# Layer 0's expert block: GpSimd's scalings and weighted sums cut into pieces that stand singly behind indirect transfers

## The chip, the cores and the metric

The kernel runs on one core of one Trainium2 chip. The metric is the device time of one execution in microseconds (us). The engines are TensorE (PE, with PEld for its weight loads), VectorE (DVE), ScalarE (ACT), GpSimd (POOL) and SyncE (SP), which issues the plain transfers. GpSimd issues the indirect ones, which send rows to places in DRAM given by a list of indices, or fetch them from there.

## The reference, cut to what matters

Two layers, each an attention part and a mixture of experts. The change touches only layer 0's experts and the normalisation behind them:

```python
h = _layernorm(x) * (1 + cb) + sb
x = x + gb * _L0_ffn_ref(h, ...)
# _L0_ffn_ref: router logits -> softmax -> top 2 of 8 experts; each expert is
# 128 -> 512, gelu, 512 -> 128; the result is the weighted sum of the two experts' rows
# layer 1 begins with
h = _layernorm(x) * (1 + ca) + sa
```

x has 4 batches of 1024 tokens with 128 channels.

## The kernel before, in words

Every engine has its own program; they meet at semaphores. The first block, `front`, does layer 0's attention, the router and the sort. Its order is written out by hand in `FRONT_ORDER`: each engine walks the same list and executes the stages that it has. GpSimd's last stages there are `sd.1.6` to `sd.1.15`, the last sends of batch 1, one indirect transfer each (line 158). VectorE's last ones are `be.1` (the choice of the two best experts), `gates`, `ix.1` (row numbers) and `te.1` (the expert of each tile), lines 767 to 823.

The second block, `experts0`, works through 92 tiles of 128 sorted rows, 23 for each of 4 batches, in 23 steps of 4 (`UNROLL`). For a tile

- SP loads the rows of 4 tiles at once (line 1292) once `rows_here` says that their batch has been sent,
- PE transposes them (line 1422), ACT copies them out (line 1399),
- DVE copies the tile's expert's up weights to a fixed place, four tiles ahead (`bring_up`, line 1335, 128x512 fp32 from SBUF to SBUF),
- PE multiplies up (line 1428), DVE adds the bias (line 1340), ACT applies gelu (line 1406), PE multiplies down (line 1435), DVE adds the second bias into `y_rows` (line 1349) and raises `y_ready`,
- SP stores two tiles of `y_rows` at once (line 1286); when the store has landed it raises `y_free`.

Beside this GpSimd works through a list of its own (lines 1307 to 1327). Batches 0 and 1 have been sent in `front` (`SENT_EARLY` is 2). For batch 2 and then batch 3 it scales and shifts the batch's normalised rows in two operations of 128x1024 (lines 149 and 151) and sends them in 16 indirect transfers (line 158). Then, for batches 0, 1 and 2, it waits until SP has stored the batch's tiles (`y_free`), fetches the rows with 16 indirect transfers (`gather`, line 1207), and, for batches 0 and 1, does the weighted sum in five operations of 128x1024 (`weighted_sum`, lines 1708 to 1723). Batch 3 is fetched, and batches 2 and 3 are summed, in the block that follows.

The transfers are paced by `next_tile`: it counts a tile number up and waits until that tile's `y_rows` are done. Its number never falls behind a batch's start:

```python
def next_tile():
    tile_at[0] += 1
    pool.wait_ge(y_ready, tile_at[0] + 2)
```

So a transfer that comes late does not wait at all, and neither do those behind it until the count has caught up.

Once a batch is summed (`summed`), DVE computes the statistics of its rows for layer 1's normalisation in two unrolled steps that begin at step `STATS_AT` (13 for batch 0, 20 for batch 1), and GpSimd raises the variance to the power -1/2 (`invert`, line 1691), which it does between transfers of the following batch. A block ends when all engines have ended.

## Time and profile before

| | us |
|---|---|
| median of 3 runs | 1414.41 (1411.29 to 1415.12) |
| profiled execution, its own time | 1412.28 |
| its span | 1410.6 |
| block `experts0` in the trace | about 186 to 403 |
| first and last tile's `y_rows` (line 1349) | 196.68 and 400.23 |

Times in the rows are microseconds from the span's start. In a timeline row the first number is the start, the second the duration; in square brackets stands the idle time of the engine before it, and what ended it. A windows row gives a stretch, its length, and the busy time of PE, PEld, DVE, ACT and POOL, each with its number of instructions, then the granted clock of TensorE (1.00 is full speed), the DMA engines' busy share and GB/s. DMA_INDIRECT is an indirect transfer's issue on GpSimd, not its landing.

### The profile page before, as it was taken

The numbers are of one execution on the slowest core, as the hardware profiler recorded it, in microseconds if no ns is written. First come the engines' busy times: TensorE is split into PE (matmuls) and PEld (weight loads), VectorE is DVE, ScalarE is ACT, GpSimd is POOL, SyncE is SP. The second block draws the span as 40 slices with busy tenths as digits, with TensorE's granted clock in tenths as the row PEclk, the third lists the DMA queues.
The fourth block names the chain that finished last, engine by engine and source line by source line (L and its number), as shares of the span: only waits on it lengthen the run. The fifth ranks groups of instructions, "written<-read, shape, count | busy, mean of one in ns | idle before, by whom it ended". The sixth has DMA issues, their size and how long they took to land. (4 is left out here: it accounts for less than half of the span.)

```text
span 1410.6 us, 28627 instructions
## 1 busy us (share of the span) xinstructions
PE 1275.9 (90%) x9145; PEld 817.9 (58%) x9146; DVE 1030.0 (73%) x2720; ACT 918.1 (65%) x1320; POOL 511.8 (36%) x608
## 2 busy tenths in 40 slices
PE   6999768989886778999999999998999989998999
PEld 3877668988863423333334433333434357778898
DVE  5656266667568669888888878888988857787554
ACT  4565523333355487888888878888888848774232
POOL 5337835466449242222201222220122200388800
PEclk9999779999988799999999999999999989999999
DMA  8980112332316722222222222222022014011211
GB/s 258 222 53 24 36 58 87 97 80 72 85 53 232 201 46 37 43 41 39 32 34 33 41 39 41 42 35 38 24 42 37 9 48 139 17 57 57 71 35 32
DMA packets 112673, 93.96 MB, mean 67 GB/s; under 512 B 20034, under 2 KB 98336, under 8 KB 112544
## 3 DMA queue, kind: packets, MB, share of 16 engines
q1 hardware_dynamic: 101192, 76.18, 25.0%
q0 software_dynamic: 6144, 12.73, 3.1%
q10 hardware_dynamic: 5208, 3.43, 1.0%
q8 instruction: 69, 1.13, 0.4%
q14 instruction: 60, 0.49, 0.1%
HBM read 50.40 MB, written 41.89 MB: 65 GB/s over the span
## 5 line engine op out<-in xcount | busy, mean ns | idle before, releaser
L2446 ACT ACTIVATE probs<-scores_ps 128x1024 f32<-128x1024 f32 x512 | 507.2, 1027 | 86.2 <-PE scores_ps L2473 81.5
L2473 PE MATMUL scores_ps<-q_pack,k_pack 64*128 64x512 f32 x1024 | 246.6, 494 | 36.1 <-ACT probs L2446 21.2
L2490 PE MATMUL pv_ps<-probs,v_pad 128*32 128x512 f32 x2048 | 275.9, 611 | 0.0
L2473 PEld LDWEIGHTS scores_ps<-q_pack,k_pack 64*128 64x128 f32 x1024 | 96.2, 185 | 309.6 <-issue 153.5
L2366 POOL TENSOR_TENSOR squares<-sparse_scores 128x512 f32<-128x512 f32 x32 | 41.0, 1280 | 474.2 <-DVE sparse_scores L2611 474.1
L1406 ACT ACTIVATE hidden_experts<-pre_experts 128x512 f32<-128x512 f32 x94 | 59.3, 631 | 130.2 <-DVE pre_experts L1340 66.5
L2683 DVE TENSOR_SCALAR_CACHE_REDUCE junk<-sparse_scores,at 128x1024 f32<-128x1024 f32 x96 | 122.8, 1279 | 3.4
L1428 PE MATMUL up_ps_experts<-x_t_experts,up_weights_now_experts 128*128 128x128 f32 x752 | 108.2, 289 | 16.4 <-issue 7.7
L1428 PEld LDWEIGHTS up_ps_experts<-x_t_experts,up_weights_now_experts 128*128 128x128 f32 x752 | 96.1, 200 | 22.6 <-DVE up_weights_now_experts L1335 11.1
L1435 PE MATMUL down_ps_experts<-weights_t,hidden_experts 128*128 x736 | 100.5, 281 | 0.2 <-issue 0.2
L1435 PEld LDWEIGHTS down_ps_experts<-weights_t,hidden_experts 128*128 128x128 f32 x736 | 92.7, 198 | 0.0
L3278 POOL DMA_INDIRECT expert_rows_dram<-expert_input_tail,send_to_tail x64 | 63.4, 991 | 79.9 <-DVE send_to_tail L3406 61.4
L1340 DVE TENSOR_TENSOR pre_experts<-up_ps_experts,weights_t 128x512 f32<-128x512 f32 x94 | 64.5, 687 | 34.8 <-PE up_ps_experts L1428 26.4
L3607 ACT ACTIVATE hidden_tail<-up_ps_tail,weights_t 128x160 f32<-128x160 f32 x128 | 41.0, 394 | 67.3 <-PE up_ps_tail L3746 61.6
L158 POOL DMA_INDIRECT expert_rows_dram<-expert_input,pick x64 | 64.0, 1000 | 51.9 <-DVE y_rows_experts L1349 31.7
L2490 PEld LDWEIGHTS pv_ps<-probs,v_pad 128*32 128x32 f32 x2048 | 40.5, 108 | 64.9 <-issue 63.8
L2539 PE MATMUL misc_ps<-sparse_v,sparse_w_t 128*128 (+1 forms) x480 | 69.5, 288 | 0.0
L2539 PEld LDWEIGHTS misc_ps<-sparse_v,sparse_w_t 128*128 128x128 f32 x480 | 58.1, 191 | 14.3 <-issue 14.3
L2611 DVE TENSOR_SCALAR_CACHE_REDUCE sparse_scores<-misc_ps 128x1024 f32<-128x1024 f32 x32 | 39.2, 1224 | 27.2 <-PE misc_ps L2510 27.1
L1335 DVE COPY up_weights_now_experts<-weights_t 128x512 f32 x96 | 57.6, 603 | 1.6 <-PEq L453 1.4
L3778 PE MATMUL out_ps_tail<-gated_out_pieces_tail,place_tail 128*128 128x128 bf16 x960 | 57.5, 221 | 0.0
L3778 PEld LDWEIGHTS out_ps_tail<-gated_out_pieces_tail,place_tail 128*128 128x128 bf16 x960 | 56.1, 99 | 0.6
(416 smaller groups left out, 2493.0 us busy)
## 6 DMA issues: line engine op xcount, KB each, us to landing
q_pack<-q_pieces_dram SPq DMA_DIRECT2D x120, 64.0 KB
k_pack<-k_pieces_dram SPq DMA_DIRECT2D x120, 64.0 KB
expert_rows_dram<-zeros SPq DMA_DIRECT2D x1, 6400.0 KB, 23.0
x_rows_experts<-expert_rows_dram SPq DMA_DIRECT2D x25, 256.0 KB
expert_rows_dram<-y_rows_experts SPq DMA_DIRECT2D x46, 128.0 KB
q_pieces_dram<-q_pieces_prep SPq DMA_DIRECT2D x8, 512.0 KB, 3.6
k_pieces_dram<-k_pieces_prep SPq DMA_DIRECT2D x8, 512.0 KB, 4.1
expert_rows_dram<-zeros SPq DMA_DIRECT2D x1, 2640.0 KB, 40.0
```

The lines of the kernel that those rows point to most:

```text
L158: pool.indirect_dma_start(self.rows, bass.IndirectOffsetOnAxis(ap=g.pick0[:, b, k, n : n + 1], axis=0), self.h[:, b * NT + n, :], None).th ...
L1340: dve.tensor_tensor(pre[:, k % 2], up_ps[k % 2][:], up_bias(e).unsqueeze(2).to_broadcast([P, FC, P]), ALU.add).then_inc(pre_ready, 1)
L1406: act.activation(hidden[:, k % 2], pre[:, k % 2], ACT.Gelu).then_inc(hidden_ready, 1)
L1428: ins = pe.matmul(up_ps[k % 2][:, c, :], up_now[:, k % UNROLL, c, :], x_t[:, k % UNROLL, :], start=True, stop=True)
L1435: ins = pe.matmul(down_ps[k % 2][:, 0:C], hidden[:, k % 2, c, :], down_w(e, c), start=(c == 0), stop=(c == FC - 1))
L2446: act.activation(probs[:, kt % 2, 2 * pair : 2 * pair + 2, c * 512 : c * 512 + 512], scores_ps[n % 2][:].rearrange("p (h t) -> p h t", h=2 ...
L2473: ins = pe.matmul(scores_ps[n % 2][:, head * 512 : head * 512 + 512], k_pack[group % 2][rows, pair, kt * P : kt * P + P].bitcast(F32R), q_ ...
L2490: ins = pe.matmul(pv_ps[32 * j : 32 * j + 32, c, :], v_pad[:, group % 2, kt, j, :], probs[:, kt % 2, j, c * 512 : c * 512 + 512], start=(k ...
L2539: ins = pe.matmul(misc[:, 0:C], w_t[:, n, :], f.sparse_v[:, bass.ds(b * NT + n, 1), :].rearrange("p n c -> p (n c)"), start=(n == 0), stop ...
L2683: step(dve.tensor_scalar(junk[:], s[:, t, :], at[:, t : t + 1], None, ALU.is_ge, ALU.add, accum_out=count[:, t : t + 1]))
L3278: pool.indirect_dma_start(expert_rows.rows, bass.IndirectOffsetOnAxis(ap=send_to[:, b, k, n : n + 1], axis=0), n3[:, b % 3, n, :], None).t ...
L3778: ins = pe.matmul(out_ps[h][:, i * C : i * C + C], place[:, (b * SLOT_TILES + t) % PLACES, n * P : n * P + P], pieces[:, (b * MIX_PARTS + ...
```

## The change

Batch 2's scaling and shifting moves to the end of `front`, in 8 pieces of 128x256 (`hq.2.0` to `hq.2.7`, behind `sd.1.15`). Batch 3's, in 8 such pieces, stands behind the first 8 sends of batch 2. The weighted sums are made of half batches: 10 operations of 128x512 for each batch. Batch 0's ten stand behind fetches 1 to 10 of batch 1. Of batch 1's ten, 8 (`ADDED_FIRST`) run in a row once batch 1 has been fetched, and two stand behind fetches 0 and 1 of batch 2. The fetches of batch 2 are paced from tile 76 (`LAST_FROM`). The statistics of batch 0 move from step 13 to step 17. Both `invert` operations move behind the last fetch and its pacing wait. Batch 1's fetches get a semaphore of their own.

```diff
+QUARTERS = 4
+    def scale_and_shift_part(self, pool, step, b, i):
+        at = b * NT + i % QUARTERS * (NT // QUARTERS)
+        h = self.h[:, at : at + NT // QUARTERS, :]
+        if i == QUARTERS:
+            step.settle()
+        op, by = ((ALU.mult, CB), (ALU.add, SB))[i // QUARTERS]
+        step(pool.tensor_tensor(h, h, bc(self.mod0[:, b, MOD0_PARTS.index(by), :], NT // QUARTERS), op))
...
-sd.1.12 sd.1.13 sd.1.14 sd.1.15 wk.10 ce2.3.1 ...
+sd.1.12 sd.1.13 sd.1.14 sd.1.15 hq.2.0 hq.2.1 hq.2.2 hq.2.3 hq.2.4 hq.2.5 hq.2.6 hq.2.7 wk.10 ce2.3.1 ...
...
+                def scale_and_shift_part(b, i):
+                    if i == 0:
+                        for h in range(2):
+                            wait_made(pool, "tu2", b, h)
+                    moe.scale_and_shift_part(pool, step, b, i)
...
-    STATS_AT = (13, 20)
+    STATS_AT = (17, 20)
+    ADDED_FIRST, LAST_FROM = 8, 76
...
                     if b >= SENT_EARLY:
-                        moe.scale_and_shift(pool, step, b)
                         step.settle()
-                        moe.send_rows(g, pool, b, apart=next_tile)
+                        for i in range(SEND_PARTS):
+                            moe.send_rows(g, pool, b, i, SEND_PARTS, apart=next_tile)
+                            if b + 1 < B and i < 2 * QUARTERS:
+                                moe.scale_and_shift_part(pool, step, b + 1, i)
...
-                for b in range(B - 1):
-                    pool.wait_ge(y_free, b * (2 * AHEAD) + (2 * AHEAD + 1))
-                    tile_at[0] = max(tile_at[0], (b + 1) * moe.tiles)
-                    gather(pool, g, picked, b, [(k, n) for k in range(2) for n in range(NT)], g.rows_picked, apart=next_tile)
-                    if 1 <= b <= EARLY:
-                        pool.wait_ge(var_ready, b)
-                        g.ln1.invert(pool, b - 1).then_inc(rstd_ready, 1)
-                    pool.wait_ge(g.rows_picked, (b + 1) * (16 * 2 * NT))
-                    if b < EARLY:
-                        for part in weighted_sum(g, picked, b, NT):
-                            part(pool, step)
+                sums = [weighted_sum(g, picked, b, NT // 2) for b in range(EARLY)]
+                def add_up(b):
+                    sums[b].pop(0)(pool, step)
+                    if not sums[b]:
                         pool.sem_inc(summed, 1)
+                def fetch(b, sem, of, behind):
+                    for i, (n, k) in enumerate([(n, k) for k in range(2) for n in range(NT)]):
+                        gather(pool, g, picked, b, [(k, n)], sem)
+                        next_tile()
+                        if i in behind:
+                            if of == 0 and i == behind[0]:
+                                pool.wait_ge(g.rows_picked, 16 * 2 * NT)
+                            add_up(of)
+                    if behind:
+                        tile_at[0] += 1
+                pool.wait_ge(y_free, 2 * AHEAD + 1)
+                tile_at[0] = max(tile_at[0], moe.tiles)
+                fetch(0, g.rows_picked, None, ())
+                pool.wait_ge(y_free, 2 * (2 * AHEAD) + 1)
+                tile_at[0] = max(tile_at[0], 2 * moe.tiles)
+                fetch(1, g.second_picked, 0, range(1, 11))
+                pool.wait_ge(g.second_picked, 16 * 2 * NT)
+                for _ in range(ADDED_FIRST):
+                    add_up(1)
+                pool.wait_ge(y_free, 3 * (2 * AHEAD) + 1)
+                tile_at[0] = max(tile_at[0], LAST_FROM)
+                fetch(2, g.rows_picked, 1, range(10 - ADDED_FIRST))
+                for b in range(EARLY):
+                    pool.wait_ge(var_ready, b + 1)
+                    g.ln1.invert(pool, b).then_inc(rstd_ready, 1)
+                pool.wait_ge(g.rows_picked, 2 * (16 * 2 * NT))
                 pool.wait_ge(rstd_ready, EARLY)
```

## Rows read from the trace of the kernel before

**Rows 1.** The page, busy time of each engine over the span

```profile
PE 1275.9 (90%) x9145; PEld 817.9 (58%) x9146; DVE 1030.0 (73%) x2720; ACT 918.1 (65%) x1320; POOL 511.8 (36%) x608
```

**Rows 2.** Windows, three stretches of the expert block

```profile
228.00:250.00 22.00, 18.16 (x141) 17.33 (x140) 12.79 (x24) 6.41 (x11) 12.95 (x11) 0.92 0.25 75
250.00:297.00 47.00, 46.84 (x413) 46.31 (x412) 30.58 (x74) 19.03 (x31) 22.70 (x24) 1.00 0.37 99
...
356.00:375.00 19.00, 15.04 (x107) 14.51 (x106) 7.66 (x18) 5.42 (x9) 9.62 (x10) 0.82 0.25 68
```

**Rows 3.** Timeline, `y_rows` of tiles 16, 24, 48, 54, 58, 64, 72, 78

```profile
228.28 0.29 DVE L1349 TENSOR_TENSOR y_rows_experts<-down_ps_experts,down_bias 128x128 f32<-128x128 f32 x1 [0.42 <-SPq L1294]
...
250.05 0.29 DVE L1349 TENSOR_TENSOR y_rows_experts<-down_ps_experts,down_bias 128x128 f32<-128x128 f32 x1 [0.47 <-SPq L1294]
...
296.77 0.29 DVE L1349 TENSOR_TENSOR y_rows_experts<-down_ps_experts,down_bias 128x128 f32<-128x128 f32 x1 [0.48 <-SPq L1294]
...
311.59 0.29 DVE L1349 TENSOR_TENSOR y_rows_experts<-down_ps_experts,down_bias 128x128 f32<-128x128 f32 x1 [0.93 <-issue]
...
326.55 0.29 DVE L1349 TENSOR_TENSOR y_rows_experts<-down_ps_experts,down_bias 128x128 f32<-128x128 f32 x1 [0.55 <-SPq L1294]
...
338.26 0.29 DVE L1349 TENSOR_TENSOR y_rows_experts<-down_ps_experts,down_bias 128x128 f32<-128x128 f32 x1 [0.46 <-SPq L1294]
...
356.23 0.29 DVE L1349 TENSOR_TENSOR y_rows_experts<-down_ps_experts,down_bias 128x128 f32<-128x128 f32 x1 [0.54 <-SPq L1294]
...
375.07 0.29 DVE L1349 TENSOR_TENSOR y_rows_experts<-down_ps_experts,down_bias 128x128 f32<-128x128 f32 x1 [0.88 <-SPq L1294]
```

**Rows 4.** Timeline, VectorE's operations beside GpSimd's, in both blocks

```profile
88.93 2.35 POOL L149 TENSOR_TENSOR expert_input<-expert_input,mod 128x1024 f32<-128x1024 f32 x1
...
89.39 1.91 DVE L752 SCALAR_TENSOR_TENSOR 0b_minus_mean_rstd_front<-ln0b_mean_var_front,ln0b_rstd_front 128x4 f32<-128x4 f32 x1
...
227.47 2.36 POOL L149 TENSOR_TENSOR expert_input<-expert_input,mod 128x1024 f32<-128x1024 f32 x1 [1.43 <-DMA expert_rows_dram<-expert_input,pick]
...
228.49 1.62 DVE L1335 COPY up_weights_now_experts<-weights_t 128x512 f32 x1
```

**Rows 5.** Windows, line 1335 alone, sum over 296.9 to 308 and 338 to 350.5

```profile
sum 23.60, DVE 15.33; mean DVE 7.67
```

**Rows 6.** Timeline, first and fifth of five sends in a row, and VectorE

```profile
232.61 1.01 POOL L158 DMA_INDIRECT expert_rows_dram<-expert_input,pick  x1 [0.28 <-POOL expert_input L151]
...
237.72 0.96 POOL L158 DMA_INDIRECT expert_rows_dram<-expert_input,pick  x1 [0.30 <-issue]
...
239.85 0.69 DVE L1340 TENSOR_TENSOR pre_experts<-up_ps_experts,weights_t 128x512 f32<-128x512 f32 x1 [3.48 <-remote]
```

**Rows 7.** Timeline, first of seven fetches in a row, and VectorE

```profile
356.28 1.04 POOL L1207 DMA_INDIRECT v<-expert_rows_dram,pick  x1 [6.98 <-SPq L1294]
...
363.55 0.29 DVE L1349 TENSOR_TENSOR y_rows_experts<-down_ps_experts,down_bias 128x128 f32<-128x128 f32 x1 [2.96 <-remote]
```

**Rows 8.** Timeline, the end of `front` and the block's first matmul

```profile
185.16 0.19 DVE L823 TENSOR_SCALAR tile_expert<-expert_front 128x46 int32<-128x46 f32 x1
...
186.08 2.33 POOL L149 TENSOR_TENSOR expert_input<-expert_input,mod 128x1024 f32<-128x1024 f32 x1 [9.68 <-POOLq L453]
...
188.72 1.11 PE L1422 MATMUL xt_ps_experts<-ident,x_rows_experts 128*128 128x128 f32 x4 [8.44 <-DMA x_rows_experts<-expert_rows_dram]
```

**Rows 9.** Timeline, GpSimd's operations of 128x512 and 128x256 elsewhere

```profile
505.36 1.04 POOL L2368 TENSOR_TENSOR squares<-squares 128x512 f32<-128x512 f32 x1
506.48 0.73 POOL L2370 TENSOR_TENSOR squares<-squares 128x256 f32<-128x256 f32 x1
```

**Rows 10.** Timeline, the end of the expert block

```profile
388.58 1.68 POOL L1691 TENSOR_TENSOR ln_rstd<-ln_var_eps,minus_half 128x8 f32<-128x8 f32 x1 [2.48 <-DVE ln_var_eps L1687]
...
400.23 0.29 DVE L1349 TENSOR_TENSOR y_rows_experts<-down_ps_experts,down_bias 128x128 f32<-128x128 f32 x1
...
403.18 0.24 DVE L1695 SCALAR_TENSOR_TENSOR ln_minus_mean_rstd<-ln_mean_var,ln_rstd 128x8 f32<-128x8 f32 x2 [2.32 <-PEq L1269]
```

More of the change, by code:

```diff
@@ L195 @@
 lg.2.1 wk.18 wt.8 lgk.2.1 h2t.3.0 wt.7 wt.4 wk.8 lg.3.0 wk.7 wt.14 lgk.3.0 wk.12 wk.14 wk.4 rs2.3.1 sd.1.6 sd.1.7 sd.1.8 sd.1.9 sd.1.10 sd.1.11
-sd.1.12 sd.1.13 sd.1.14 sd.1.15 wk.10 ce2.3.1 no2.3.1 tu2.3.1 h2t.3.1 lg.3.1 lgk.3.1 be.1 po.1 exps gates ix.1 te.1
+sd.1.12 sd.1.13 sd.1.14 sd.1.15 hq.2.0 hq.2.1 hq.2.2 hq.2.3 hq.2.4 hq.2.5 hq.2.6 hq.2.7 wk.10 ce2.3.1 no2.3.1 tu2.3.1 h2t.3.1 lg.3.1 lgk.3.1 be.1 po.1 exps gates ix.1 te.1
 """
@@ L635, in _ @@
                         h2=scale_and_shift,
+                        hq=scale_and_shift_part,
                         sd=send,
@@ L1482, in __init__ @@
         self.rows_picked = a.sem("rows_picked")
+        self.second_picked = a.sem("second_rows_picked")
         self.zeros = a.sb("zeros", [P, C])
```

## The prediction, made before the changed kernel was run

> **What bounds the kernel now.** The page comes first: TensorE is busy for 90% of the span and GpSimd for 36% [rows 1], so GpSimd's work costs time only where it makes others wait. Next the windows over the expert block. Between 250 and 297 us, where GpSimd only issues transfers, PE is busy for 46.84 of 47 us at full clock: the stretch is PE's. Between 228 and 250 PE lacks 3.8 us and between 356 and 375 4.0 us, and its clock is at a mean of 0.92 and 0.82 there [rows 2]. So the block has places where PE is kept waiting.
>
> To size them I count tiles by VectorE's `y_rows`. Tiles 24 to 48 take 296.77 - 250.05 = 46.72 us, or 1.947 us a tile; this is the pace with paced transfers beside it [rows 3]. Against it:
>
> - tiles 16 to 24: 21.77 us for 15.57, **6.2 lost**. Batch 3's two scalings stand at its start, five sends in a row behind them.
> - tiles 48 to 54: 14.82 for 11.68, **3.15 lost**, beside batch 0's weighted sum; tiles 54 to 58: 14.96 for 7.79, **7.15 lost**, beside nine fetches in a row.
> - tiles 64 to 72: 17.97 for 15.57, **2.4 lost**, beside batch 1's weighted sum.
> - tiles 72 to 78: 18.84 for 11.68, **7.15 lost**, beside seven fetches in a row, which begin when SP's store lets GpSimd go [rows 3, 7].
>
> That is 26.05 us in four places. Two things cost them, and the timeline separates them.
>
> *A long operation of GpSimd holds VectorE.* The copy of up weights takes 1.62 us from 228.49; it ends 0.28 us after GpSimd's operation that began at 227.47 and took 2.36 [rows 4]. A copy that starts while GpSimd computes waits for the end of that one operation and slips in ahead of the next. Beside the two sums 11 copies take 15.33 us, 1.39 each instead of 0.42 [rows 5], and the tiles lose (3.15 + 2.4) / 11 = 0.50 us: 0.97 of delay costs 0.50, so some 0.45 is swallowed. By length, ten whole operations of 2.36 us cost 5.55 us, 0.235 us for each us of GpSimd's computing. The two scalings come to 2 x 2.36 x 0.235 = 1.1 us by this, which leaves 6.2 - 1.1 = 5.1 us for the five sends.
>
> *A run of transfers goes with a stall.* From 232.61 to 237.72 five sends start 1.28 us apart, and VectorE stands for 3.48 us for "remote", until 239.85 [rows 6]; in the run of seven it stands for 2.96 us until 363.55 [rows 7]. All three runs of five or more in this block have this, the runs of three or fewer don't. I can't name the mechanism, only the coincidence. TensorE's clock is low behind each one, part of the price.
>
> **The change, part by part.**
>
> *Batch 3's scaling in pieces behind batch 2's sends.* What stood at 227.47 goes, and with it the reason for the run of five: GpSimd comes to batch 3's sends on time and paces them. Minus 6.2. In its place 8 pieces of 128x256 come in tiles 0 to 8. One takes 0.73 us and a gap of 0.08, the distance between the end of one operation and the next [rows 9]; a send with its gap takes 1.28 [rows 6]. Together 2.09 us for a tile of 1.947, so GpSimd falls 1.1 us behind over 8 and catches up with two or three sends in a row. A piece meets a copy in a third of the tiles and holds it for half its length: 0.15 us on average, less than is swallowed. I take +0.5 in all, bounds 0 and, by length, 8 x 0.73 x 0.235 = 1.4.
>
> *Batch 2's scaling moved to the end of `front`.* GpSimd is idle there for 9.68 us before 186.08 [rows 8], and 8 x 0.81 = 6.5 us fit, so GpSimd isn't late. The cover isn't free, though. In these same 9 us VectorE goes through the chain of small operations that ends at 185.16 and ends the block [rows 8]. A small operation with two inputs in SBUF took 1.91 us from 89.39 and ended 0.02 us after GpSimd's operation of 2.35 us [rows 4]. If each two-input operation waits so for a piece, and one of them slips in between two, the chain can be walked by the code's list: six pieces each catch one operation of `be.1`, which then ends 2.5 us late (the reductions between them run freely), and two more meet the first of `gates`. The chain ends 3.1 us late. Bounds: 0 if VectorE gets through, 8 x 0.73 = 5.8 if it waits for every piece in full. I take +3.1. What goes at the head of `experts0` saves nothing: there PE waits 8.44 us for the rows' load, until 188.72 [rows 8], not for the copies.
>
> The Trainium skill, in "SBUF — State Buffer", section on the two physically separate sides, says that the port pair shared by VectorE and GpSimd is an exclusive lock held for a whole instruction, and that a VectorE operation with two SBUF inputs takes part. By this rule the term is 3.1, and it speaks against putting the pieces under that chain; the one row alone would also allow a value near 0.
>
> *Batch 0's weighted sum in ten pieces behind batch 1's fetches.* The sum at 296 goes (-3.15) and the run of nine behind it (-7.15). A piece of 128x512 takes 1.04 [rows 9] to half of 2.36, 1.18 [rows 4]; with gaps ten make 12 us, and ten fetches 12.8: 24.8 us for ten tiles of 19.5. Batch 1's fetches also begin some 2 us behind tile 47, because the store of its rows must land. So at the tenth piece GpSimd is 7 us, more than three tiles, behind, and fetches 11 to 15 follow each other without pause: a fetch gains 0.67 us on a tile, not enough for the pacing to return before the last. **A run of five is left.** The nearest row is the run of five sends, 5.1 us; bounds 0 and the 7.15 of the run of seven. I take +5.1. The pieces themselves: GpSimd computes half of the time, so a copy waits 0.3 us on average, and 0.45 is swallowed; I take +1.0 for ten tiles, bounds 0 and, by length, 11.8 x 0.235 = 2.8.
>
> *Batch 1's sum, eight pieces in a row, two behind fetches.* Minus 2.4. Nine us of pieces lie over 5 tiles; a copy waits half a piece, 0.6 us, instead of 0.97. By what is swallowed that is 0.15 a tile, by length 0.45; I take +1.2 with the two later pieces, bounds 0.3 and 2.8. Is `summed` in time? Piece 9 starts with tile 76's `y_rows`, then a fetch, then piece 10: 0.3 + 1.3 + 1.3 + 1.3 = 4.2 us, tile 78.2. VectorE asks in tile 80, over 3 us later: no wait.
>
> *Batch 2's fetches paced from tile 76.* They begin at the same store, but after the first one GpSimd waits for tile 76, and then one tile each: the run of seven is gone. Minus 7.15. What is late next is the last fetch: it goes out with tile 90 and lands before the block's end.
>
> *Both powers at the end.* GpSimd now waits for the last `y_rows`, 400.23 + 0.29, is released some 0.3 later, and does two powers of 1.68 us: 404.2 [rows 10]. Before, the last store ended the block: 2.66 us from the end of `y_rows` to VectorE's next operation at 403.18 [rows 10]. The passage from one block to the next takes some 0.5 us, if I take the one before, from 185.35 to 186.08, less GpSimd's start [rows 8]. So the block ends at 404.7: **+1.5**, bounds 0.9 and 2.2.
>
> *Statistics at step 17 instead of 13*: the same operations on VectorE in other tiles, `summed` long there (about tile 62, asked at 68). Nothing. SP's list isn't touched.
>
> **Sum.** Removed 6.2 + 10.3 + 2.4 + 7.15 = 26.05. Added 3.1 + 0.5 + 5.1 + 1.0 + 1.2 + 1.5 = 12.4. Gain 13.65 against the profiled execution's own 1412.28: 1398.6. That execution lies 2.1 us under the median of the runs shown, so I say **1399**.
>
> **Rivals.**
>
> 1. *The remaining run of five is free.* For it: the next block fetches twelve in a row without a "remote" wait. Against: three of three in this block. 1394.
> 2. *Pieces cost by their length.* 8 x 0.73 + 20 x 1.18 = 29.4 us of pieces at 0.235 make 6.9 instead of 2.7. For it: without pauses GpSimd loses its phase against the copies. 1403.
> 3. *The stalls aren't the runs' doing* and merely move. Then two of 7.15 come back: 1399 + 14.3 = 1413, no difference. For it: no row names who releases VectorE.
> 4. *Neither the pieces in `front` nor the run cost anything*: 1399 - 3.1 - 5.1 = 1391.
> 5. *Slower.* With GpSimd never idle for 20 tiles, each copy is held by a piece and again by the next. It decides from (13.65 + 4.2) / 20 = 0.9 us a tile above what I count, so about 1.0, twice what whole operations cost. At 1.2 it gives 1421.
>
> **Chances.** My sum 0.45, its own range 1395 to 1403 (bounds of the front and the pieces). Rival 1 0.2, rival 2 0.15, rival 3 0.1, rival 4 0.07, rival 5 0.03. The range leaves out rivals 3 and 5: 1390 to 1409. A measurement of this kernel can't tell less than about 0.3%, 4.2 us, from no change. Faster by more: 0.87. Within: 0.10 (rival 3). Slower: 0.03.
>
> **What would show it.** In the profile after: the block begins near 189; no run of five sends and no "remote" wait before tile 60; tiles 16 to 24 take 15.6 us and 48 to 58 about 20.5; then five fetches in a row near tiles 61 to 65, with one wait of 3 us and a low clock; tiles 72 to 78 take 11.7; GpSimd's two powers are the block's last work. I am wrong if the "remote" waits stay in number with no run before them, if the chain from `be.1` to `te.1` isn't longer, or if copies beside pieces take over 1.2 us as a rule.

## The result, and the profile after

The changed kernel takes 1409.57 us (median of 19 runs, 1404.37 to 1411.89) where the kernel before takes 1412.7 on the same chip (19 runs, 1408.88 to 1417.26). The ratio is 0.9978, 95% interval 0.9968 to 0.9989: some 3 us faster, clear of the scatter but under the 0.3% that the prediction took as the least that can be told from no change. The prediction said 1399 and a range of 1390 to 1409. It is wrong, narrowly outside its range and by three quarters of its gain. One profiled execution below, that of `e5_wait_alone`, is a slow one (PE busy for 2919.5 us with the instructions that took it 1275.9 before), so its times are far from the others' and only what doesn't hang on TensorE is read from it.

The timeline of the changed kernel, `y_rows` of tiles 16, 24, 48, 54, 58, 64, 72, 78 as in [rows 3], and of tile 84:

```profile
232.43 0.29 DVE L1392 TENSOR_TENSOR y_rows_experts<-down_ps_experts,down_bias 128x128 f32<-128x128 f32 x1 [0.42 <-SPq L1312]
...
248.95 0.29 DVE L1392 TENSOR_TENSOR y_rows_experts<-down_ps_experts,down_bias 128x128 f32<-128x128 f32 x1 [0.44 <-SPq L1312]
...
296.43 0.29 DVE L1392 TENSOR_TENSOR y_rows_experts<-down_ps_experts,down_bias 128x128 f32<-128x128 f32 x1 [0.51 <-SPq L1312]
...
308.36 0.29 DVE L1392 TENSOR_TENSOR y_rows_experts<-down_ps_experts,down_bias 128x128 f32<-128x128 f32 x1
...
317.77 0.29 DVE L1392 TENSOR_TENSOR y_rows_experts<-down_ps_experts,down_bias 128x128 f32<-128x128 f32 x1
...
332.81 0.29 DVE L1392 TENSOR_TENSOR y_rows_experts<-down_ps_experts,down_bias 128x128 f32<-128x128 f32 x1 [0.80 <-SPq L1312]
...
349.89 0.29 DVE L1392 TENSOR_TENSOR y_rows_experts<-down_ps_experts,down_bias 128x128 f32<-128x128 f32 x1 [0.84 <-SPq L1312]
...
361.85 0.29 DVE L1392 TENSOR_TENSOR y_rows_experts<-down_ps_experts,down_bias 128x128 f32<-128x128 f32 x1 [0.74 <-SPq L1312]
...
377.99 0.29 DVE L1392 TENSOR_TENSOR y_rows_experts<-down_ps_experts,down_bias 128x128 f32<-128x128 f32 x1 [0.78 <-SPq L1312]
```

In the kernel before, tile 84's row stands at

```profile
387.04 0.29 DVE L1349 TENSOR_TENSOR y_rows_experts<-down_ps_experts,down_bias 128x128 f32<-128x128 f32 x1 [0.84 <-SPq L1294]
```

Subtract neighbours: tiles 16 to 24 take 16.5 us where [rows 3] gives 21.8, 54 to 58 take 9.4 for 15.0, 72 to 78 take 12.0 for 18.8. All of that was forecast, within 1 us. But 58 to 64 take 15.0 for 11.7, and 78 to 84 take 16.1, where the kernel before took 12.0. GpSimd's timeline there, and VectorE's, show what stands beside it:

```profile
362.98 0.96 POOL L1224 DMA_INDIRECT v<-expert_rows_dram,pick  x1 [0.81 <-POOL x L1767]
364.24 0.95 POOL L1224 DMA_INDIRECT v<-expert_rows_dram,pick  x1 [0.30 <-issue]
365.50 0.95 POOL L1224 DMA_INDIRECT v<-expert_rows_dram,pick  x1 [0.30 <-issue]
366.76 0.95 POOL L1224 DMA_INDIRECT v<-expert_rows_dram,pick  x1 [0.31 <-issue]
...
368.87 0.69 DVE L1383 TENSOR_TENSOR pre_experts<-up_ps_experts,weights_t 128x512 f32<-128x512 f32 x1 [1.78 <-remote]
```

Four fetches follow each other without a pause, and "remote" stands behind them again. GpSimd had fallen behind with pieces 9 and 10 and was catching up.

Now the block's end, GpSimd's and VectorE's timeline, beside [rows 10]:

```profile
390.53 0.95 POOL L1224 DMA_INDIRECT sparse_v<-expert_rows_dram,pick  x1 [1.53 <-DVE y_rows_experts L1392]
391.19 0.29 DVE L1392 TENSOR_TENSOR y_rows_experts<-down_ps_experts,down_bias 128x128 f32<-128x128 f32 x1
391.57 3.40 POOL L1735 TENSOR_TENSOR ln_rstd<-ln_var_eps,minus_half 128x8 f32<-128x8 f32 x2
402.10 0.24 DVE L1739 SCALAR_TENSOR_TENSOR ln_minus_mean_rstd<-ln_mean_var,ln_rstd 128x8 f32<-128x8 f32 x2 [10.28 <-PEq L1287]
402.73 1.64 POOL L1224 DMA_INDIRECT v<-expert_rows_dram,pick  x1 [7.76 <-POOLq L1287]
```

The last rows are ready 9.0 us earlier than before (391.19 for 400.23), but the next block begins only 1.1 us earlier (402.10 for 403.18). From the end of the last `y_rows` to VectorE's next operation, the *passage*, it is 10.6 us in place of 2.66. GpSimd's powers end at 394.97; the 7.13 us behind them hold nothing on any engine.

So the account is: tile 0 begins 3.2 us later, the 91 tiles behind it take 191.3 us in place of 203.55 (12.2 less), the passage takes 8.0 more. The block ends 1.1 us sooner. The other 2.4 us of the span's difference (1407.1 to 1410.6) lie in later blocks, which the change doesn't touch; they are scatter, for that rest of the span takes anything from 1000.7 to 1008.0 us in the traces of this case.

### The profile page after: what moved, and what is told of

Read it like the earlier page. It is cut to its first block and busy times, and to the rows that moved or that the text cites. A ratio compares the mean times of both kernels' runs of the same rounds, so it can differ in the third digit from the quotient of the medians.

```text
span 1407.1 us, 28652 instructions
## 1 busy us (share of the span) xinstructions
PE 1267.5 (90%) x9145; PEld 809.4 (58%) x9146; DVE 1026.6 (73%) x2720; ACT 918.4 (65%) x1320; POOL 517.4 (37%) x630
## 5 line engine op out<-in xcount | busy, mean ns | idle before, releaser
L1378 DVE COPY up_weights_now_experts<-weights_t 128x512 f32 x96 | 52.2, 546 | 1.6 <-PEq L463 1.4
```

## The experiments

Theories. **P**: the powers at the end are what the passage pays for. **L**: GpSimd's coming late to the block's end costs, whatever it does there. **R**: stalls go with runs of transfers, not with long operations.

### First set: where the powers stand, the front, pacing alone

The kernel before takes 1411.11 us in this set. `e1_powers_inside` and `e2_one_power_last`:

```
-fetch(2, g.rows_picked, 1, range(10 - ADDED_FIRST))
+fetch(2, g.rows_picked, 1, range(10 - ADDED_FIRST), {5: 0, 13: 1})   # e1: power 0 behind fetch 5, 1 behind 13
+fetch(2, g.rows_picked, 1, range(10 - ADDED_FIRST), {5: 0})          # e2: power 1 at the end
```

> The changed kernel with both powers moved back between fetches of batch 2 (behind fetch 5 and fetch 13); GpSimd's last act in the block is again the wait for the last tile. In the changed kernel 10.6 us pass from the end of the last y_rows to the next block's first operation, 2.7 before. Theory P (the two powers, 3.4 us in the trace, hold the block's end and something comes on top of them): the passage falls to 2.7 us, the time by 8 us against the changed kernel, ratio to before about 0.992. Theory L (GpSimd comes to the block's end late, and a fixed 7 us of its own follow its last act, whatever that was): the passage falls only by the 3.4 us, to 7.2, ratio about 0.9955. Theory N (the passage is a matter of other engines): 10.6 us stay, ratio 0.998.

> The changed kernel with batch 0's power behind fetch 5 and only batch 1's at the end. Theory P with a price for each power: passage halfway, about 6.6 us. Theory L: 10.6 - 1.7 = 8.9 us. Ratio to before 0.995 and 0.997.

Measured: e1 1406.95 us, ratio 0.9972 (0.9957 to 0.9986), passage 9.7; e2 1407.32, 0.9964 (0.9949 to 0.9979), passage 9.0. The timeline of e1, last fetch, last `y_rows` and VectorE's next operation:

```profile
390.53 0.96 POOL L1224 DMA_INDIRECT sparse_v<-expert_rows_dram,pick  x1 [0.30 <-issue]
390.56 0.29 DVE L1395 TENSOR_TENSOR y_rows_experts<-down_ps_experts,down_bias 128x128 f32<-128x128 f32 x1
...
400.57 0.24 DVE L1742 SCALAR_TENSOR_TENSOR ln_minus_mean_rstd<-ln_mean_var,ln_rstd 128x8 f32<-128x8 f32 x2 [9.39 <-PEq L1287]
```

With no power at the end at all the passage loses 0.9 of its 8.0 us. P falls. For L, e2's passage came as expected (8.9), but e1's is 2.5 us above the expected 7.2; the second set shows why.

`e3_front_undone` takes the eight `hq.2` pieces out of `front` and scales batch 2 whole at the head of `experts0`, as before.

> The changed kernel with batch 2's scaling back at the head of the expert block as two whole operations; nothing of it in the front. In the changed trace VectorE's chain from its copy of the logits to the last operation takes 12.9 us, 10.6 before. My theory: the chain is 10.6 us again, 2.3 us gained; at the block's head the four copies are held again (5.1 us for 1.6), which costs 0 to 0.4. Against the changed kernel -2 us, ratio to before 0.9965. Rival (the chain's length is hidden behind PE or the load): no difference, 0.998.

Measured: 1405.59, ratio 0.9958 (0.9942 to 0.9973). VectorE's chain, from the operation behind `top`'s reduction to the end of `tile_expert`, takes 9.81 us as in the kernel before; in the changed kernel, with the pieces beside it, 12.15. The passage stays at 10.9. The interval just overlaps that of the changed kernel (0.9968 to 0.9989), so the time alone doesn't show a gain; the chain does.

`e4_pacing_alone` is the kernel before, long operations and all, with its waits moved:

```
+tile_at[0] = max(tile_at[0], SENDS_FROM[b])      # {2: 0, 3: 19}
-tile_at[0] = max(tile_at[0], (b + 1) * moe.tiles)
+tile_at[0] = max(tile_at[0], FETCHES_FROM[b])    # (34, 54, 73)
```

> The kernel before with nothing moved and nothing cut: only the tile numbers of the pacing are set to where GpSimd really comes, 19 for batch 3's sends and 34, 54 and 73 for the fetches. Theory R (runs of transfers carry the stalls): no run over two, no remote waits, minus 5 + 7 + 7 us and the 1 us of the run of three at tile 34, less 1 us of powers: 17 to 19 us faster, ratio 0.987. Theory S (the long operations of GpSimd carry them, the runs being only what stands behind): the stalls stay, under 4 us gained, ratio 0.997 to 1.0. Of the change's own parts (pieces) nothing is in it.

Measured: 1405.82, ratio 0.9963 (0.9945 to 0.9981), as good as the change. Against 1.927 us a tile (the pace of tiles 24 to 32 in every trace here; the prediction's 1.947 holds a little loss), tiles 16 to 24 lose 1.4 in place of 6.35 and 54 to 58 lose 0.9 in place of 7.25, though the long scalings and the whole sum stand ahead of them. That speaks for R. But R expected 17 to 19 us, and 5.3 came. Tiles 72 to 78 still lose 5.2, since a run was left: the second sum ends at 354.99, past tile 73, and five fetches follow each other behind it. GpSimd's and VectorE's timeline:

```profile
355.81 1.04 POOL L1207 DMA_INDIRECT v<-expert_rows_dram,pick  x1 [0.82 <-POOL x L1725]
...
360.92 0.95 POOL L1207 DMA_INDIRECT v<-expert_rows_dram,pick  x1 [0.30 <-issue]
...
363.09 0.29 DVE L1351 TENSOR_TENSOR y_rows_experts<-down_ps_experts,down_bias 128x128 f32<-128x128 f32 x1 [2.93 <-PE down_ps_experts L1437]
```

And tiles 48 to 54 lose 9.0 in place of 3.3: GpSimd's first sum ends at 308.24, and VectorE, by then at step 13, waits for it:

```profile
308.32 0.49 DVE L1675 BATCH_NORM_STATS2 ln_stats<-x 128x6 f32<-128x128 f32 x2 [7.12 <-POOLq L1328]
```

A faster stretch of tiles brings the fixed step 13 to a sum that hasn't moved; so the later statistics of the change aren't free to leave out.

### Second set: the block's end, and doses of runs

The kernel before takes 1411.53 us here. `e5_wait_alone` is the kernel before with one line more, and `e8_late_fetch` holds its last fetch back:

```
+pool.wait_ge(y_ready, 2 + B * moe.tiles)      # e5, at GpSimd's end
 pool.wait_ge(rstd_ready, EARLY)

+pool.wait_ge(y_ready, 1 + B * moe.tiles)      # e8, ahead of the last of batch 2's 16 fetches
```

> The kernel before, with one wait more on GpSimd, at the end of its part of layer 0's expert block: it waits for the last tile's rows. No transfer and no operation is moved. Theory A (any late step of GpSimd costs a fixed price at the block's end): from the last tile's y_rows to the next block's first VectorE operation some 7 to 9 us in place of 2.7, time +5 to +6 us, about 1418. Theory B (only real work of GpSimd near the end costs, a vector operation or an indirect transfer, by what has to be finished or fetched behind it): the passage stays at 2.7 to 3.5 and the time at 1411 to 1413.

> The kernel before, with the last of the sixteen fetches of batch 2 held back until tile 91's rows are there; everything else of GpSimd, both powers too, is done before it. Theory A: as with the wait alone, passage 7 to 9. Theory B: passage about 9 to 10 us (the fetch ends 1.5 us behind tile 91, and 9.1 us lay between the end of the last fetch and the next block in the run with both powers inside), where the wait alone gives 3; time +7 us, about 1419. Theory C (the price is that of the powers or of a vector operation alone): passage 3 to 4.5, time 1412 to 1414.

Measured: e5 1415.63, ratio 1.0026 (1.0006 to 1.0045); e8 1418.8, ratio 1.0056 (1.0035 to 1.0076). VectorE's timeline of e5 at the block's end, far later than elsewhere since its tiles took 5.06 us each:

```profile
868.37 0.29 DVE L1350 TENSOR_TENSOR y_rows_experts<-down_ps_experts,down_bias 128x128 f32<-128x128 f32 x1 [1.66 <-PE down_ps_experts L1436]
...
875.79 0.24 DVE L1696 SCALAR_TENSOR_TENSOR ln_minus_mean_rstd<-ln_mean_var,ln_rstd 128x8 f32<-128x8 f32 x2 [6.79 <-PEq L1269]
```

868.66 to 875.79 is 7.13 us, where it was 2.66 without the wait. Nothing else was added: no operation, no transfer. The 4.5 us agree with the 4.1 of the medians. In e8 two things are not as the expectation says: power 1 stands behind the held fetch, not ahead of it, and the wait is for tile 90's rows, not tile 91's (`y_ready` begins at 2). GpSimd's and VectorE's timeline:

```profile
402.04 1.68 POOL L1695 TENSOR_TENSOR ln_rstd<-ln_var_eps,minus_half 128x8 f32<-128x8 f32 x1
410.85 0.24 DVE L1699 SCALAR_TENSOR_TENSOR ln_minus_mean_rstd<-ln_mean_var,ln_rstd 128x8 f32<-128x8 f32 x2 [8.95 <-PEq L1269]
```

403.72 to 410.85 is 7.13 again (the passage is 9.3). With GpSimd's last operation as the zero, or in e5 the last `y_rows` that it waits for, the next block began 7.13 us later in the changed kernel, 7.13 in e5, 7.13 in e8, 7.12 in e2, 7.14 in e4, 7.45 in e3. Why e3 has 0.3 more is not known. In the kernel before GpSimd was done at 390.26 [rows 10]; 7.13 more is 397.4, hidden behind the tiles. **Theory L holds, as a rule for this block: the next block begins at the later of (GpSimd's last event + 7.13) and (last `y_rows` + 2.66).** In e1 the last event is the landing of the last fetch, which no row of e1 gives; by the rule it is 400.57 - 7.13 = 393.4, some 2 us behind the end of that fetch's row and 2.9 behind its start. Where landings were traced (`e9_both_mended`), a fetch lands 2.5 to 3.2 us behind its start. The Trainium skill, in "Perfetto Trace Analysis", section on the DMA instruction from GpSimd, says that the profile's end of such an instruction is when its descriptors are made, not when the data has moved; the trace agrees: in e9 rows of 0.94 to 1.09 us stand beside those 2.5 to 3.2 us.

`e6_fetches_early` is the changed kernel with an earlier GpSimd: ten pieces of batch 1's sum ahead of the fetches, these from tile 73, four of them in three tiles.

```
-ADDED_FIRST, LAST_FROM = 8, 76
+ADDED_FIRST, LAST_FROM = 10, 73
-next_tile()
+if b < 2 or i % 4 != 3:
+    next_tile()
...
-fetch(2, g.rows_picked, 1, range(10 - ADDED_FIRST))
+fetch(2, g.rows_picked, None, ())
```

> The changed kernel, with all ten pieces of batch 1's sum ahead of batch 2's fetches (they fit into the 9 us in which GpSimd waited for the rows), the fetches from tile 73 and four of them in three tiles, so that GpSimd is done with the fetches at about tile 86 and with both powers about 6 us before tile 91. If both readings hold (the run of four fetches at tiles 79 to 82 cost 4.2 us; the late end of GpSimd cost 8.0 us): tiles 78 to 84 lose 0.4 to 1 in place of 4.6, the passage is 2.7 in place of 10.6, time 1409.6 - 12 = 1397 to 1398. If the passage is not about GpSimd's lateness: passage 10 to 11 and 1405. If the stall at tile 79 is not about the run of transfers but about that place in the block: 78 to 84 still lose 4 to 5, and 1401.

Measured: **1400.92, ratio 0.9927 (0.9902 to 0.9951)**. GpSimd's powers, and VectorE's timeline at the end:

```profile
377.40 3.53 POOL L1736 TENSOR_TENSOR ln_rstd<-ln_var_eps,minus_half 128x8 f32<-128x8 f32 x2
...
389.07 0.29 DVE L1393 TENSOR_TENSOR y_rows_experts<-down_ps_experts,down_bias 128x128 f32<-128x128 f32 x1
...
392.02 0.24 DVE L1740 SCALAR_TENSOR_TENSOR ln_minus_mean_rstd<-ln_mean_var,ln_rstd 128x8 f32<-128x8 f32 x2 [2.32 <-PEq L1287]
```

The passage is 2.66 again, all 8 us are back. Tiles 72 to 84 lose 5.2 us, no less than in the changed kernel (5.0): three runs of three fetches (from 353.27, 362.0 and 368.5) have taken the place of one run of four. That part of the expectation missed, by 3 to 4 us, and so did the total. The total is the one that the expectation names for a stall that belongs to the place and not to the run. The tiles say otherwise in part: 72 to 78 lose 2.3 where the changed kernel, without a run there, loses 0.4, and 78 to 84 lose 2.9 for its 4.6.

`e7_dose_of_runs` is the changed kernel with batch 0's fetches in runs of 2, 3, 4 and 7, a pause behind each:

```
-next_tile()
+if b > 0:
+    next_tile()
+elif i in RUNS:                    # {1: 2, 4: 3, 8: 4}
+    tile_at[0] += RUNS[i]
+    next_tile()
```

> The changed kernel, with batch 0's sixteen fetches (tiles 32 to 48, nothing else of GpSimd beside them) sent in runs of 2, 3, 4 and 7 with a pause after each, where the changed kernel paces them by tiles. If length of an unbroken run is what stalls: the run of 2 costs 0, of 3 about 1 us, of 4 about 3.5 to 4, of 7 about 7, in all some 11 to 12 us over tiles 32 to 50 in place of 1.4, each with a wait of VectorE for PE's results of 2 to 3 us or more. If it is the number of transfers in a stretch whatever their order: no more than 1 to 2 us in all. If each transfer beyond the second costs the same (about 1.2 us): 1.2, 2.4 and 6, in all 9 to 10.

Measured in one execution: 1414.75. Losses of the tiles beside and behind each run: 0.6 for the 2 (tiles 32 to 34), 1.1 for the 3 (34 to 36), 1.8 for the 4 (38 to 42), 5.2 for the 7 (42 to 46). The first is no price of a run: the same two tiles lose 0.6 to 1.2 in the changed kernel, e1, e2, e3 and e6, which have no run in them, and so they do in the kernel before (0.7). The other three places lose 0.1 at most in all of these. So runs of three and more do make the loss, in a stretch where GpSimd computes nothing, and longer ones cost more per transfer; but less than I expected from the changed kernel's two runs of four. The run of seven, GpSimd's and VectorE's timeline:

```profile
288.01 0.94 POOL L1224 DMA_INDIRECT sparse_v<-expert_rows_dram,pick  x1 [6.24 <-DVE y_rows_experts L1397]
...
295.50 1.15 POOL L1224 DMA_INDIRECT sparse_v<-expert_rows_dram,pick  x1 [0.30 <-issue]
...
295.21 0.29 DVE L1397 TENSOR_TENSOR y_rows_experts<-down_ps_experts,down_bias 128x128 f32<-128x128 f32 x1 [3.99 <-PE down_ps_experts L1483]
...
298.17 0.69 DVE L1388 TENSOR_TENSOR pre_experts<-up_ps_experts,weights_t 128x512 f32<-128x512 f32 x1 [2.33 <-PE up_ps_experts L1476]
```

### Third set: everything mended, and a surprise

`e9_both_mended` is the changed kernel with e3's front and

```
-STATS_AT = (17, 20)
-ADDED_FIRST, LAST_FROM = 8, 76
+STATS_AT = (16, 19)
+ADDED_FIRST, LAST_FROM = 10, 73
 add_up(of)
+if of == 0 and i == behind[-1]:
+    tile_at[0] += 2
```

power 0 behind fetch 5 (the sixth) and power 1 behind the last fetch, and no wait behind fetch 7 of batch 2. `e10_front_kept` keeps the front pieces. `e11_paced_without_pieces` is e4 with `FETCHES_FROM = (34, 54, 76)` and `STATS_AT = (17, 20)`.

> The changed kernel with what the runs so far found at fault taken out: batch 2 is scaled whole at the head of the block as before (no pieces in front of it); two tiles of pause behind the tenth piece of batch 0's sum, so that no run of four follows; all ten pieces of batch 1's sum ahead of batch 2's fetches, these from tile 73 with one tile skipped, power 0 behind the sixth and power 1 behind the last fetch's issue. Law of the block's end (the next block begins 7.13 us behind GpSimd's last wait or operation, or 2.66 us behind tile 91's rows, whichever is later): GpSimd is done some 4 us before tile 91 ends or earlier, passage 2.7 to 3.5. Runs: tiles 58 to 64 lose 0.3 to 1 in place of 3.5, 72 to 84 lose 1.5 in place of 5.0. Together with 2 to 3 us of the front: 1392 to 1395. If the stalls only move to another place when a run is taken out: 1397 to 1400.

> The same kernel with the change's eight front pieces of batch 2's scalings kept. If they cost net what the first look said (start of tile 0 later by 1.5 to 3 us, nothing saved in tiles 0 to 16 because the sends there are paced by tiles anyway): 2 to 3 us above the other kernel of this call, about 1396. If their place is worth something (sends of batch 2 begin sooner, so tile 23 has its rows sooner): equal or below it.

> The kernel before with no piece at all, only its waits moved: batch 3's sends from tile 19, the fetches from tiles 34, 54 and 76, the statistics from step 17 on in place of 13. Theory (runs of transfers are the stall, and what the pieces buy is GpSimd's time near the block's end): tiles 0 to 91 take 192 to 194 us, some 10 below before, as with the pieces; but the third set of fetches can't begin before tile 76 without a run, so GpSimd's last wait is for tile 91, the passage is 9 to 10 us and the time 1406 to 1408. If the pieces themselves removed the stalls (the long operations were the stall): tiles take 197 to 203 and the time is 1412 or more.

Measured: e9 1388.39, e10 1390.33, e11 1397.14. These look splendid, until one reads the kernel before beside them: **1390.85 us** in this set, on another chip, 20 us below all earlier ones. The ratios are 0.9984 (0.9968 to 0.9999), 1.0001 (0.9988 to 1.0014) and 1.0047 (1.0030 to 1.0064). In e11's trace ten fetches stand in one run from 357.53 on, and VectorE waits for no other compute engine for as long as 1.6 us in the block. Beside each other, e9 and e10 differ by 1.9 us, the price of the front's pieces, but their intervals overlap.

I call a chip where the kernel before takes 1411 to 1413 us *stalling* (the first result, e1 to e8), one where it takes 1391 to 1393 *quiet* (e9 to e18, on three chips). Each set ran on one chip. Whether it is the chips that differ or the time at which the sets ran, these runs don't tell; no stalling one came up again.

### Fourth set: the same kernels on a quiet chip

`e12_before_again` and `e13_after_again` are the two kernels of this case unchanged, `e14_mended_again` is e9, `e15_paced_again` is e11.

> The kernel before, unchanged, on the chip of this call. If the chip is one with stalls (kernel before at 1411 us): tiles 0 to 91 take 203 to 204 us with VectorE waits of 2 to 4 us behind the runs of five and seven transfers. If it is one without (1391 us): some 186 to 188 us and no such wait, the runs standing there all the same; passage 2.66 in both.

> The changed kernel, unchanged. On a chip with stalls: 0.2% faster than before, as first measured. On a chip without: tiles take some 3 to 4 us less than before's (the long scalings and sums with their held copies are gone), the front costs 3.2 and the block's end 8.0, so 6 to 9 us or 0.4 to 0.6% slower than before.

> The kernel with both faults mended (front scalings whole, no run of four, GpSimd done before the last tile). On a chip with stalls: tiles 0 to 91 in 183 to 187 us, passage 2.7, 1393 to 1396 where before takes 1411, 1.0 to 1.3% faster. On a chip without: 0.16% faster as in the last call, 1388 beside 1391.

> The kernel without pieces, its waits moved. On a chip with stalls: 1403 to 1407 beside 1411 (its run of ten transfers at the third set of fetches stalls, the passage is 9 us). On a chip without: 0.5% slower, as in the last call.

Measured, beside 1391.83 of the kernel before: **the changed kernel 1399.14, ratio 1.0065 (1.0035 to 1.0095), slower**; e14 1390.21, 0.9984 (0.9971 to 0.9996); e15 1397.96, 1.0040 (1.0029 to 1.0052). The kernel before on the quiet chip (e12, one execution more, 1393.43), GpSimd's and VectorE's timeline, the run of fetches that stalled in [rows 7]:

```profile
345.25 1.04 POOL L1207 DMA_INDIRECT v<-expert_rows_dram,pick  x1 [6.98 <-SPq L1294]
...
352.88 0.95 POOL L1207 DMA_INDIRECT v<-expert_rows_dram,pick  x1 [0.31 <-issue]
...
352.88 0.29 DVE L1349 TENSOR_TENSOR y_rows_experts<-down_ps_experts,down_bias 128x128 f32<-128x128 f32 x1 [0.49 <-SPq L1294]
...
359.16 0.95 POOL L1207 DMA_INDIRECT sparse_v<-expert_rows_dram,pick  x1 [0.31 <-issue]
```

Here it grows to twelve, since the tiles no longer stop and GpSimd takes longer to come level with its pacing; VectorE's waits in it are of at most 1.2 us, for SP's store. Its `y_rows` of tiles 16, 24, 48, 54, 58, 64, 72, 78:

```profile
228.67 0.29 DVE L1349 TENSOR_TENSOR y_rows_experts<-down_ps_experts,down_bias 128x128 f32<-128x128 f32 x1 [0.42 <-SPq L1294]
...
245.50 0.29 DVE L1349 TENSOR_TENSOR y_rows_experts<-down_ps_experts,down_bias 128x128 f32<-128x128 f32 x1 [0.42 <-SPq L1294]
...
292.15 0.29 DVE L1349 TENSOR_TENSOR y_rows_experts<-down_ps_experts,down_bias 128x128 f32<-128x128 f32 x1 [0.53 <-SPq L1294]
...
306.95 0.29 DVE L1349 TENSOR_TENSOR y_rows_experts<-down_ps_experts,down_bias 128x128 f32<-128x128 f32 x1 [0.95 <-SPq L1294]
...
315.89 0.29 DVE L1349 TENSOR_TENSOR y_rows_experts<-down_ps_experts,down_bias 128x128 f32<-128x128 f32 x1 [1.72 <-SPq L1294]
...
327.25 0.29 DVE L1349 TENSOR_TENSOR y_rows_experts<-down_ps_experts,down_bias 128x128 f32<-128x128 f32 x1 [0.45 <-SPq L1294]
...
345.20 0.29 DVE L1349 TENSOR_TENSOR y_rows_experts<-down_ps_experts,down_bias 128x128 f32<-128x128 f32 x1 [0.53 <-SPq L1294]
...
357.26 0.29 DVE L1349 TENSOR_TENSOR y_rows_experts<-down_ps_experts,down_bias 128x128 f32<-128x128 f32 x1 [1.21 <-SPq L1294]
```

Both kernels on both kinds of chip give a table of losses against 1.927 us a tile (difference of two such rows, less 1.927 for each tile), from one trace each. I take what a quiet chip loses as VectorE's copies held by GpSimd's operations, and the rest as stalls; no run separates the two otherwise:

| tiles | before, stalling | before, quiet | after, stalling | after, quiet |
|---|---|---|---|---|
| 0 to 16 | 0.8 | 0.8 | 1.7 | 0.8 |
| 16 to 24 | 6.35 | 1.4 | 1.1 | 0.0 |
| 24 to 48 | 0.5 | 0.4 | 1.2 | 0.3 |
| 48 to 54 | 3.3 | 3.2 | 0.4 | 0.3 |
| 54 to 58 | 7.25 | 1.2 | 1.7 | 1.7 |
| 58 to 64 | 0.15 | -0.2 | 3.5 | 1.7 |
| 64 to 72 | 2.55 | 2.5 | 1.7 | 1.7 |
| 72 to 78 | 7.3 | 0.5 | 0.4 | 0.4 |
| 78 to 84 | 0.4 | 0.5 | 4.6 | 0.8 |

Over tiles 0 to 91 the kernel before takes 203.55 us on the stalling chip and 185.46 on the quiet one, the changed one 191.3 and 182.8. So, by that reading, the change takes 9.6 us of stalls out where there are any, and 2.7 us of holding everywhere. Its passage costs 8.0 us more on both. The rule of the block's end holds on the quiet chip too; the changed kernel (e13), GpSimd's and VectorE's timeline:

```profile
382.50 3.40 POOL L1735 TENSOR_TENSOR ln_rstd<-ln_var_eps,minus_half 128x8 f32<-128x8 f32 x2
393.03 0.24 DVE L1739 SCALAR_TENSOR_TENSOR ln_minus_mean_rstd<-ln_mean_var,ln_rstd 128x8 f32<-128x8 f32 x2 [10.28 <-PEq L1287]
```

385.90 to 393.03: 7.13. The next block begins there at 385.46 in the kernel before, 7.6 us sooner, and the medians differ by 7.3.

### Last sets: the mended kernel on a stalling chip, not reached

`e16_mended_third` is e9. `e17_power_in_the_gap` and `e18_mended_last` are e9 with `power(0)` ahead of the wait for batch 2's rows.

> The mended kernel. If the chip is one with stalls (kernel before at 1411): tiles 0 to 91 in 184 to 188 us, since a run of five is left at tile 80 (2 to 4 us) and runs of three at tiles 8, 16 and 32; passage 2.66; 1393 to 1396, ratio 0.987 to 0.990. If it is one without: ratio 0.9984 a third time.

> The mended kernel with power 0 moved into GpSimd's wait for the rows ahead of batch 2's fetches, so that the run of five behind it becomes one of three at most. With stalls: 2 to 4 us below the other kernel of this call, 1390 to 1393. Without: equal to it within 1 us.

> The mended kernel with power 0 in the gap. On a chip with stalls (kernel before at 1411): 1390 to 1393, ratio 0.985 to 0.988. On one without (1391): ratio 0.997 to 0.998 as before.

Both sets fell on quiet chips (kernel before at 1392.98 and 1391.3). e16: 1388.81, ratio 0.9977 (0.9961 to 0.9994). e17: 1389.05, 0.9972 (0.9958 to 0.9987). e18: 1390.17, 0.999 (0.9973 to 1.0006). The best version is thus e9 with or without the moved power, 0.1 to 0.3% ahead of the kernel before on a quiet chip; that is less than 0.3% each time, and e18's interval takes in 1. On a stalling chip its value is not measured; e6, which has less of the mending, was 0.7% ahead there.

## Why the prediction was wrong

By its own steps. All signs of the tile terms were right and most sizes good; two steps failed.

- **"Both powers at the end ... The passage from one block to the next takes some 0.5 us ... +1.5": the step that failed.** Measured +8.0. I read the one passage before (0.5 to 1.4 us) as what a block's end costs, but there GpSimd had been idle for 9.68 us [rows 8] and so paid nothing visible. That the next block comes 7.13 us behind a late GpSimd is shown by e5 (a wait alone) and e6 (an early GpSimd takes all 8.0 us away), on a quiet chip by e13 and e14 (passage 10.6 and 2.66). The powers have only 0.9 us of it (e1). The cause stands one step earlier: the pacing wait behind the sixteenth fetch, from tile 76, waits for tile 91.
- **"The run of seven is gone. Minus 7.15"** was right for tiles 72 to 78 (7.3 to 0.4), but the step said that fetches then follow one tile each. I had worked out in the paragraph before that piece 10 ends at tile 78.2, and didn't go on: two pieces and two fetches take 5 us from tile 76, and GpSimd catches up with four fetches in a row. Tiles 78 to 84 lose 4.2 us more than before on the stalling chip. It was the same reasoning that I had used to find the run behind batch 0's sum.
- *"A run of five is left", +5.1*: it is a run of four, and tiles 58 to 64 lose 3.5, of which 1.7 are pieces (the quiet chip's loss). Right in mechanism, too dear by 3.
- *Ten pieces beside tiles 48 to 58, +1.0*: on the quiet chip tiles 48 to 64 lose 3.7 with the pieces and 4.3 without. So pieces hold copies nearly as the whole sum does. The size was wrong by 2.7, near the bound "by length" of 2.8; that part of rival 2 was right. The eight pieces at tiles 64 to 72: 1.7 for my 1.2.
- *Batch 3's scalings, minus 6.2 and plus 0.5*: 5.2 less on the stalling chip in tiles 16 to 24, 1.0 more in tiles 0 to 16. Of the 6.35 there, 1.4 are holding and 4.9 stall, beside my 1.1 and 5.1.
- *Front, +3.1*: tile 0 came 3.2 us later, but by chance. VectorE's chain is longer by 2.3 us. The changed kernel's timeline, GpSimd's pieces and VectorE's operations with two inputs beside them:

```profile
178.06 5.90 POOL L161 TENSOR_TENSOR expert_input<-expert_input,mod 128x256 f32<-128x256 f32 x8
...
178.32 0.69 DVE L794 SCALAR_TENSOR_TENSOR of_best_front<-chosen_front,shifted_front 128x128 f32<-128x128 f32 x1
...
179.78 0.70 DVE L800 TENSOR_TENSOR code_front<-code_front,expert_rank 128x128 f32<-128x128 f32 x1
...
181.23 0.76 DVE L806 TENSOR_TENSOR selected_front<-chosen_front 128x128 bf16<-128x128 f32 x1
```

  All three take 0.29 us in the kernel before. I take it that they wait for a piece, though each for less of one than I counted. What the prediction drew from the Trainium skill, "SBUF — State Buffer", the section on the two separate sides, an exclusive lock on the port pair shared by VectorE and GpSimd, came out on that rule's side (2.3 us), not on the side of 0. Of the 3.2 us, 1.2 were there ahead of the pieces: `top`'s reduction starts at 176.42 for 175.22. Over all traces tile 0 comes at 196.8 us on average in the twelve without pieces in the front (195.6 to 198.4) and at 199.1 in the seven with them (198.4 to 200.0), e5's left out: a price of 2.3 us. e10 against e9 puts it at 1.9. *"So GpSimd isn't late"* holds in five of these seven; in e6 and e13 GpSimd's end, not VectorE's, decides when the block begins, which is the failed step over again at the front.
- *Statistics at step 17, nothing*: right, and needed (e4).
- *Rivals*: 3 said that the stalls aren't the runs' doing and merely move. e7 shows that runs make them; e11 and e12 show that a run isn't enough, since runs of seven to fifteen cost no stall on a quiet chip. My sentence that I could name "only the coincidence" was fair, but I gave 19.4 of 26.05 us to it and no rival in which a run's price is absent on some chips.

Where the gain went, for the stalling chip: predicted 13.65 us; 6.5 of it were lost at the block's end, 4.2 at tiles 78 to 84. That leaves 3.0, which is near the 3.1 of the medians by chance: in the two traces the block ends only 1.1 us sooner, and the 1.9 between are the balance of the sizes above.

## What to carry to other kernels

Before work of an engine is moved to a block's end, find when that engine is done now and what it has as slack; an end that costs nothing in the trace may only be hidden, and one added wait in an experiment shows its price. When a queue that paces itself is given more work, follow its debt to the last item: the catching up is a burst, here at two places. And compare with the kernel before on the same chip: the largest costs of this profile, some 18 us in the block, were absent on others, and a change tuned against them turned from 0.2% faster to 0.65% slower.

## What the runs showed of the hardware

- **GpSimd leaves a block late.** 7.12 to 7.14 us pass from its last operation, or from a bare wait, to the next block's start at the end of `experts0` in nine traces, 7.45 in a tenth (e3). At the end of `front` it is 4.01 us in the two traces where GpSimd was last (e6 and e13, from the eighth piece's end, 184.41 and 185.41, to GpSimd's next send at 188.42 and 189.41). Where VectorE is last it is 2.66 and 1.39 us. What GpSimd does in that time, and why the two ends differ, no row shows.
- **Stalls behind runs of indirect transfers exist on some chips or at some times and not at others**, at 20 us of the whole, 18 of them in this block. On a stalling chip they rise with the run: nothing to be seen for 2, then 1.1, 1.8 and 5.2 us for 3, 4 and 7 (e7, one execution). VectorE takes PE's results up 2 to 4 us late. In the kernel before, PE's product for the addition that stands at 239.85 in [rows 6] is

```profile
236.43 1.16 PE L1428 MATMUL up_ps_experts<-x_t_experts,up_weights_now_experts 128*128 128x128 f32 x8
```

  It ends at 237.59, 2.3 us before. The granted clock is low over such a stretch, 0.92 from 228 to 250 in [rows 2]; a window over tiles 16 to 24 of the kernel before on the quiet chip gives

```profile
229.00:245.00 16.00, 14.99 (x131) 14.56 (x131) 12.23 (x23) 5.61 (x9) 12.72 (x11) 1.00 0.32 98
```

  PE is busy for 14.99 of 16 us at full clock. What differs between the chips, and what holds the signals up, stays open.
